# Attention and a mixture of experts on one core: the second half of the queries in two groups of 512 in place of four of 256, their row maxima spread differently, and the last four tiles finished one by one

## The reference

```python
xn  = (x - mean) / sqrt(var + 1e-5)
# attention, one head of width 128, scale 1/sqrt(8)
q, k, v = split(xn @ w_qkv.T)
att = softmax(q @ k.T * scale) @ v @ w_proj.T + b_proj
# experts: 8, each row goes to 2 of them
t = xn @ W_in + b_in
probs = softmax(t @ W_gate + b_gate);  top 2, renormalised
mid  = relu(t @ W1[e] + b1[e])           # 128 -> 512
eout = mid @ W2[e] + b2[e]               # 512 -> 128
ffn  = (sum over the 2 experts of gate * eout) @ W_out + b_out
out  = x + att + ffn
```

## Time and profile before

| | |
|---|---|
| median of 3 runs | 240.3 us (240.28 to 240.36) |
| the profiled execution | 240.15 us |
| its span, first to last record | 238.1 us |
| PE, DVE, ACT, POOL busy in the span | 227.0, 137.3, 111.0, 140.9 us |
| granted TensorE clock | full in all 40 slices |

### The profile page before, as it was taken

How to read it: one execution, slowest core, us unless ns; L and a number is a source line. 1 busy time by engine, 2 the same in 40 slices (tenths; PEclk the granted TensorE clock), 3 DMA queues, 4 the chain that set the end, 5 groups by cost and what they waited for, 6 DMA issues and landing times.

```text
span 238.1 us, 4830 instructions
## 1 busy us (share of the span) xinstructions
PE 227.0 (95%) x1724; PEld 215.1 (90%) x1724; DVE 137.3 (58%) x334; ACT 111.0 (47%) x265; POOL 140.9 (59%) x163
## 2 busy tenths in 40 slices
PE   8899988999999999899999999999899999999985
PEld 8787876899999997899999999999899899999983
DVE  4978795652551541444444444444677885985652
ACT  2572432424325334344444444444656656566561
POOL 3149005888888850355666665563178888888710
PEclk9999999999999999999999999999999999999999
DMA  6799910111111103022222222221111112213111
GB/s 182 285 320 342 323 44 28 49 37 47 34 44 47 44 33 88 25 61 71 71 66 70 77 71 70 76 66 37 33 47 34 44 36 80 43 36 88 53 38 44
DMA packets 23047, 19.54 MB, mean 82 GB/s; under 512 B 3280, under 2 KB 19696, under 8 KB 22768
## 3 DMA queue, kind: packets, MB, share of 16 engines
q1 hardware_dynamic: 20000, 14.71, 20.3%
q0 software_dynamic: 2048, 4.20, 6.4%
q10 hardware_dynamic: 976, 0.33, 0.5%
HBM read 10.97 MB, written 8.26 MB: 81 GB/s over the span
## 4 chain that ended last, share of the span: by engine, by line
PE 57%; POOL 21%; DVE 7%; issue 7%; DMA 5%; ACT 1%; ACTq 1%; POOLq 0%; DVEq 0%
PE ps L1088 15%; PE ps L1074 15%; POOL slots_in L360 12%; POOL wtab L387 4%; POOL x_sb L333 3%; DVE part_max L611 2%; PE ps L890 2%; PE ps L963 2%; PE ps L829 2%; PE ps L964 2%; PE ps L967 2%; DMA w_raw<-in_L_attn_w_proj_dram 2%; PE ps L830 2%; PE ps L831 2%; PE ps L1062 2%
## 5 line engine op out<-in xcount | busy, mean ns | idle before, releaser
L350 POOL COPY wst<-wtab 128x1156 f32 x39 | 44.9, 1151 | 36.0 <-DVE y_sb L759 36.0
L460 ACT ACTIVATE pf<-ps 128x512 f32<-128x512 f32 x64 | 38.1, 595 | 34.5 <-PE ps L831 31.0
L611 DVE TENSOR_REDUCE part_max<-ps 128x1 f32<-128x1024 f32 x32 | 38.9, 1223 | 11.4 <-PE ps L890 10.4
L387 POOL DMA_INDIRECT wtab<-slots_out,slots x32 | 34.5, 1077 | 16.0 <-DMA slots_out<-y_sb 8.4
L360 POOL DMA_INDIRECT slots_in<-hl,slots x32 | 31.5, 984 | 20.1 <-DVE slots L691 13.2
L751 DVE TENSOR_SCALAR mid<-ps,wst 128x128 f32<-128x128 f32 x78 | 23.8, 347 | 33.3 <-PE ps L1074 33.3
L1088 PE MATMUL ps<-wst,mid 128*128 128x128 f32 x312 | 41.3, 275 | 0.7 <-DVE x_sb L638 0.7
L829 PE MATMUL ps<-q_hi,xnT_hi 128*128 128x256 f32 x128 | 41.4, 323 | 0.5 <-ACT q_hi L446 0.5
L1074 PE MATMUL ps<-xgT,wst 128*128 128x128 f32 x312 | 41.3, 275 | 0.0
L1088 PEld LDWEIGHTS ps<-wst,mid 128*128 128x128 f32 x312 | 38.0, 192 | 0.8 <-ACT mid L504 0.8
L1074 PEld LDWEIGHTS ps<-xgT,wst 128*128 128x128 f32 x312 | 38.0, 192 | 0.1
(11 more groups left out here) (158 smaller groups left out, 341.5 us busy)
## 6 DMA issues: line engine op xcount, KB each, us to landing
wtab<-in_L_ffn_W_dram SPq DMA_DIRECT2D x16, 256.0 KB, 6.0
xg<-slots_in SPq DMA_DIRECT2D x39, 64.0 KB, 1.9
slots_out<-y_sb SPq DMA_DIRECT2D x39, 64.0 KB, 1.5
slots_in<-wst SPq DMA_DIRECT2D x2, 1024.0 KB, 5.0
x_sb<-in_L_attn_x_dram SPq DMA_DIRECT2D x4, 256.0 KB, 4.7
out_dram<-x_sb SPq DMA_DIRECT2D x3, 256.0 KB
wtab<-in_L_ffn_b_dram SPq DMA_DIRECT2D x1, 512.0 KB, 7.4
slots_in<-hl,slots POOLq DMA_INDIRECT x32
```

The source lines that it names most:

```text
L350: pool.tensor_copy(wst[:, t % 4, :], wtab[:, bass.ds(experts[t], 1), :].rearrange("p a n -> p (a n)")).then_inc(Z["staged"], 1)
L387: pool.indirect_dma_start(out=z[:, j, c, :], out_offset=None, in_=slots_out, in_offset=bass.IndirectOffsetOnAxis(ap=slots[:, c, j:j + 1], ...
L460: act.activation(pf[:, i % 3, :], ps[:, st_bank(i), :], ACT.Exp).then_inc(Z["pf_done"], 1)
L611: dve.tensor_reduce(part_max[:, g % 2, m // 2, m % 2:m % 2 + 1], ps[:, b:b + 2, :], AX.XY, ALU.max).then_inc(Z["max_read"], 1)
```

## The change

Groups 4 to 7 (256 queries, 8 steps each) become groups 4 and 5 (512 queries, 16 steps each). The number of steps behind the experts stays 32, and so does the number of pairs in the whole kernel (32); a step's six score products of 256 columns become three of 512, and so do those of `values`. The eight pairs of group 4 are now all made in the steps of group 3, one to a step and two in its last; their `max_row` and `row` stand beside expert tile 3. Behind the experts eight pairs are left where twelve were. `combine(j)` and the blocks have new steps: `combine` 14 and 15 and the last block's transposes stand behind all `values`. The last group's tiles (four instead of two) are scaled, projected and added one at a time, each onto its share of the experts' product in the same PSUM bank, and DVE copies `cT` there instead of ACT.

```diff
@@ -36,11 +36,11 @@
-    GROUPS = [(256 * g, 256) for g in range(8)]
+    GROUPS = [(256 * g, 256) for g in range(4)] + [(1024, 512), (1536, 512)]
     PRE = 4
     WHOLE = 4
-    PAIR_STEP = [[2, 4, 5, 6]] + 6 * [[1, 2, 4, 5]] + [[]]
+    PAIR_STEP = [[2, 4, 5, 6]] + 2 * [[1, 2, 4, 5]] + [[1, 2, 3, 4, 5, 6, 7, 7], [1, 3, 5, 6, 8, 9, 11, 12], []]
     NG = len(GROUPS)
     SIZE = [n for _, n in GROUPS]
     CH = [BK // n for n in SIZE]
@@ -72,9 +72,9 @@
     def weighed_at(s):
-        return [j for j in range(NT) if 4 + (13 * (j + 1)) // 8 == s]
-    BLOCK_AT = {14: 0, 22: 1, 26: 2, 31: 3}
+        return [j for j in range(NT) if 5 + (31 * j) // 16 == s]
+    BLOCK_AT = {14: 0, 21: 1, 28: 2}
     ctx = ExitStack()
     with ctx:
@@ -216,11 +216,12 @@
             return ps[:, b:b + 2, 0:2 * HW].rearrange("p b (j n) -> p b j n", n=HW)
         def row_bank(c):
-            return (MA, 0)[c]
+            return (MA, 0, 1, 2)[c]
         def sum_bank(c):
-            return (MB, 1)[c]
+            return (MB, MX + 1, MA, 0)[c]
         def y_bank(t):
             return UB if t % 2 == 0 else MB
@@ -277,11 +278,15 @@
                 store_y(t)
             ov = out.rearrange("o (p j) e -> p (o j) e", p=P)
-            cuts = [TB * r for r in range(NR)] + [GROUPS[NG - 1][0] // P, NT]
+            cuts = [TB * r for r in range(NR)]
             for a, b in zip(cuts, cuts[1:]):
                 sp.wait_ge(Z["moe_added"], (b - 1) // TB + 1)
                 sp.wait_ge(Z["x_added"], sum(q < P * b for q, _ in GROUPS))
                 sp.dma_start(ov[:, a:b, :], x_sb[:, a:b, :]).then_inc(Z["stored"], 16)
+            for c in (2, 4):
+                sp.wait_ge(Z["last_added"], c)
+                a = NT - TB + c - 2
+                sp.dma_start(ov[:, a:a + 2, :], x_sb[:, a:a + 2, :]).then_inc(Z["stored"], 16)
             sp.wait_ge(Z["stored"], 16 * (NR + 1))
         @block.gpsimd
@@ -478,7 +483,7 @@
                     copy_u(g - 1)
             def before(g, k):
-                if k == STEPS[g] - 1 and g + 1 < NG:
+                if k == STEPS[g] - 1 and g + 1 < NG and g != PRE - 1:
                     row(g + 1)
             for g in range(PRE):
@@ -516,6 +521,8 @@
                     mid_relu(t + 1)
                 else:
                     step(BASE_B)
+                if t == 3:
+                    row(PRE)
             def cT_copy(b):
                 act.wait_ge(Z["cT_done"], b + 1)
@@ -800,27 +807,36 @@
                         combine(j)
                     if s - 1 in BLOCK_AT:
                         moe_add(BLOCK_AT[s - 1])
+            for j in range(NT):
+                if j not in [q for s in range(LAST - BASE_B) for q in weighed_at(s)]:
+                    combine(j)
+            dve.wait_ge(Z["cT_done"], NR)
+            dve.wait_ge(Z["wo_done"], NR - 1)
+            dve.tensor_copy(cT[:, :], ps[:, MX, :]).then_inc(Z["cT_copied"], 1)
             def last_scale(c):
-                n = FIRST_ROUND[NG] - 1
+                n = FIRST_ROUND[NG - 1]
                 dve.wait_ge(Z["out_done"], n + 1 + c)
-                link("rinv", dve.reciprocal(rinv[:, n % 2, c:c + 1], ps[:, row_bank(c), D:D + 1]))
-                dve.tensor_scalar(o_sb[:, n % 2, c, :], ps[:, row_bank(c), 0:D], rinv[:, n % 2, c:c + 1], None,
+                link("rinv", dve.reciprocal(rinv[:, c // 2, c % 2:c % 2 + 1], ps[:, row_bank(c), D:D + 1]))
+                dve.tensor_scalar(o_sb[:, c // 2, c % 2, :], ps[:, row_bank(c), 0:D], rinv[:, c // 2, c % 2:c % 2 + 1], None,
                                   ALU.mult).then_inc(Z["o_ready"], 1)
             def last_add(c):
-                at = x_sb[:, NT - 2 + c, :]
-                dve.wait_ge(Z["proj_done"], FIRST_ROUND[NG] + c)
-                return dve.tensor_tensor(at, ps[:, sum_bank(c), 0:D], at, ALU.add)
-            dve.wait_ge(Z["proj_done"], FIRST_ROUND[NG] - 1)
+                at = x_sb[:, NT - TB + c, :]
+                dve.wait_ge(Z["proj_done"], FIRST_ROUND[NG - 1] + c + 1)
+                dve.tensor_tensor(at, ps[:, sum_bank(c), 0:D], at, ALU.add).then_inc(Z["last_added"], 1)
+            dve.wait_ge(Z["proj_done"], FIRST_ROUND[NG - 1])
+            dve.wait_ge(Z["x_biased"], 1 + NT)
             last_scale(0)
             last_scale(1)
-            dve.wait_ge(Z["wo_done"], NR)
-            at = x_sb[:, NT - TB:NT - 2, :]
-            dve.tensor_tensor(at, ps[:, MX + 1, 0:2 * D].rearrange("p (j e) -> p j e", e=D), at, ALU.add).then_inc(Z["moe_added"], 1)
+            last_scale(2)
             last_add(0)
-            last_add(1).then_inc(Z["x_added"], 1)
+            last_scale(3)
+            last_add(1)
+            last_add(2)
+            last_add(3)
         @block.tensor
         def _(pe):
@@ -975,10 +991,7 @@
                 pe.wait_ge(Z["ut_copied"], g + 1)
                 if n >= 1:
                     pe.wait_ge(Z["o_ready"], n)
-                if g == PRE - 1:
-                    pe.wait_ge(Z["row_ready"], PRE + 1)
-                else:
-                    pe.wait_ge(Z["q_lo_ready"], min(NG, g + 3))
+                pe.wait_ge(Z["q_lo_ready"], PRE + 1 if g == PRE - 1 else min(NG, g + 3))
                 for k in range(2):
                     at = P * (2 * r + k)
                     last = pe.matmul(ps[:, MA, (D + 2) * k:(D + 2) * (k + 1)], ut[:, at:at + P], wvT[:, :], start=True, stop=True)
@@ -1089,8 +1102,8 @@
                                      start=(c == 0), stop=(c == HC - 1))
                 last.then_inc(Z["y_done"], 1)
+            values(BASE_B - 2)
             xg_transpose(0)
-            values(BASE_B - 2)
             xg_transpose(1)
             values(BASE_B - 1)
             layer1(0)
@@ -1109,6 +1122,9 @@
                 if t == 1:
                     for r in range(ROUNDS[PRE - 1]):
                         project(PRE - 1, r)
+                if t == 3:
+                    pe.wait_ge(Z["o_ready"], FIRST_ROUND[PRE])
+                    max_row(PRE)
                 layer2(t)
             def moe_transpose(b, pairs):
@@ -1149,25 +1165,25 @@
                         after(g, k)
             values(LAST - 2)
             values(LAST - 1)
-            pe.wait_ge(Z["cT_copied"], NR)
+            moe_transpose(NR - 1, FIRST_PAIR[NG])
+            n = FIRST_ROUND[NG - 1]
+            pe.wait_ge(Z["pf_done"], LAST)
             pe.wait_ge(Z["x_added"], NG - 1)
-            pe.wait_ge(Z["pf_done"], LAST)
-            for c in range(2):
-                at = P * (TB - 2 + c)
-                pe.matmul(ps[:, sum_bank(c), 0:D], cT[:, at:at + P], wo_sb[:, :], start=True, stop=False)
-            for c in range(2):
+            for c in range(TB):
                 pe.wait_ge(Z["ut_copied"], NG + c)
                 pe.matmul(ps[:, row_bank(c), 0:D + 2], ut[:, P * c:P * (c + 1)], wvT[:, :], start=True, stop=True
                           ).then_inc(Z["out_done"], 1)
+            pe.wait_ge(Z["cT_copied"], NR)
             pe.wait_ge(Z["moe_added"], NR - 1)
-            for j in range(TB - 2):
-                last = pe.matmul(ps[:, MX + 1, P * j:P * (j + 1)], cT[:, P * j:P * (j + 1)], wo_sb[:, :], start=True, stop=True)
-            last.then_inc(Z["wo_done"], 1)
-            for c in range(2):
-                n = FIRST_ROUND[NG] - 1
+            for c in range(TB):
+                if c >= 2:
+                    pe.wait_ge(Z["o_ready"], n + c - 1)
+                pe.matmul(ps[:, sum_bank(c), 0:D], cT[:, P * c:P * (c + 1)], wo_sb[:, :], start=True, stop=False)
+            for c in range(TB):
                 pe.wait_ge(Z["o_ready"], n + 1 + c)
-                pe.matmul(ps[:, sum_bank(c), 0:D], o_sb[:, n % 2, c, :], wpT[:, :], start=False, stop=True
+                pe.matmul(ps[:, sum_bank(c), 0:D], o_sb[:, c // 2, c % 2, :], wpT[:, :], start=False, stop=True
                           ).then_inc(Z["proj_done"], 1)
```

2 lines of the change are left out of this document (1 added, 1 removed).

## The result

The changed kernel takes **240.8 us** (20 executions, 240.34 to 242.12) where the kernel before takes 240.3 on the same chip (20 executions, 240.01 to 240.72): ratio 1.0035, interval 1.0022 to 1.0049. It is slower by about 0.5 us; forecast were 241.2 and "slower". The 20 times fall in two groups, 12 from 240.34 to 240.99 and 8 from 241.59 to 242.12; the times of before have no second group. The profiled execution took 240.99 us, of the lower group, with a span of 239.2.

What follows compares the result with a forecast made beforehand. Two chains from the experts' end, TensorE's 64 us and GpSimd's 55 us, meet in the last block. Transposes at 231.5 plus a 5.0 tail give 236.5, +0.9; span 239.0 plus 2.05 is 241.05, median 241.2, range 239.9 to 242.4.

Steps and rivals of the forecast that it cites:

- Before the experts, +3.25: Before the experts: four more pairs in group 3's steps, new waits, wider projection, no max_row; +3.25 us, between +2.3 and +3.7.
- The three new waits: Group 3's last step: second pair waits 0.64 us, first transpose waits for the last reduction, second for ScalarE's copy, 0.70.
- Beside tile 3, +0.45: Beside expert tile 3: four transposes of 128 columns add 0.45 us to TensorE; ScalarE's copy of the row is hidden.
- The list of gathers: GpSimd's list behind the experts starts 3.7 us later, so its last weighing ends at 231.0 instead of 227.32.
- the rival in which the gathers quicken: Behind the experts: slow gathers vanish, 2.5 us go, TensorE alone decides; time 239.9 us, chance 0.15.
- the one in which weighings lengthen: GpSimd and VectorE collide more: half of the 16 weighings become like the longest, chain grows 3.3 us; 244.5, chance 0.05.
- TensorE behind the experts, -5.1: Behind the experts: wider products, fewer pairs, projections and rounds save TensorE 5.1 us; its values end at a stated 231.1.
- the waits cancel: TensorE behind the experts: 3.9 us of waits and slow restarts before, 3.6 counted after, so nearly no change.
- Where both meet: Last block: combine(15) can start at 231.1, last transposes at 231.5; TensorE has been free since 231.1.
- The tail, +5.0: From the last transposes to the last addition: about 5.0 us (4.5 to 5.6), against 5.77 before.
- Sum: Whole kernel: last addition at 236.5 against 235.62, +0.9; span 239.0, with 2.05 around it 241.05; time 241.2 us.
- the rival in which the gathers no longer decide: Same rival as the gathers quickening: TensorE alone decides, values done at about 230.1; time 239.9 us, chance 0.15.

Runs made afterwards that it cites:

- Experiments 1 and 2: Changed kernel with four of eight pairs before the experts cut to 128 columns: 237.96 us; with both last values of group 3 ahead of the first expert transpose: 239.63 us.
- experiment 11: Changed kernel with only the last copy of cT on ScalarE instead of VectorE: 240.71 us, ratio 1.0024.
- experiment 6: Changed kernel without GpSimd's multiplications by the first gate; GpSimd fills a tile of its own after each pair of gathers: 238.21 us, ratio 0.9916.
- experiment 12: Changed kernel with transposes of tiles 12 to 14 ahead of the wait for combine(15) and repeated four times: 240.43 us, ratio 1.0009.

## Why the prediction was right, point by point

The sign, the size and the mechanism held; the terms, one by one:

- **Before the experts, +3.25.** Measured 96.01 - 92.47 = 3.54, of which 0.13 is there already when group 3 starts its first step. The three new waits came as described, 0.45, 0.55 and 0.46 us. Experiments 1 and 2 show that this stretch passes to the end nearly one for one.
- **Beside tile 3, +0.45.** The four transposes took 0.44 from start to start of their neighbours. The first gather came at 175.92, forecast "near 175.7".
- **The list of gathers.** Ends at 231.49, forecast 231.0: 0.25 from its start and 0.22 from its length. The right length is in part luck. The 32 gathers took 33.3 us and not 34.5 (mean 1040 ns against 1077 in the earlier trace rows), 1.2 less; the 16 weighings took 12.35 us together and not 11.57 (median 760 ns against 637), 0.8 more; and the wait for the last rows to land was 1.89 and not 1.08, 0.8 more. So half of the rival in which the gathers quicken (2.5 us) and a quarter of the one in which weighings lengthen (3.3) came true and nearly cancelled. I didn't try what lengthens a weighing.
- **TensorE behind the experts, -5.1.** Mis-sized. The forecast's own terms give 232.65 + 3.7 - 5.1 - 0.3 = 230.95 and not the 231.1 that it states. `values` ended at 232.00 - 1.61 = 230.39, although the stage began 0.25 later than forecast: 0.8 us sooner than the terms say. A product of 512 columns takes 0.227 us from start to start, not 0.23 to 0.234: three of them are 0.68 and not 0.70, which over the 63 half steps is 1.3 us more. The pitch was taken from a pair, whose two products include the change from and to other operands. The waits were named wrongly: the copy of U held `values` for 0.76 (forecast 1.2), one pair waited 0.90 (forecast 1.0 behind `combine(1)`, and a share of another 1.0), the last `low` took 0.24 (0.35). That is 1.9 of the 3.6 that were counted. The rest is slow restarts: if I add up by how much the distances between starts exceed 0.227, 0.120 and 0.110 us (512, 256 and at most 130 columns), waits and restarts come to some 4.1 us here, without the wait for `combine(15)`, and to some 4.5 before. So "the waits cancel" held in the sum (-0.4, forecast -0.3) and not in the parts. Some 0.6 us the other way is left in pairs, projections and short products, which I didn't follow one by one.
- **Where both meet.** TensorE idle for `combine(15)` just before the last transposes, as forecast, but for 1.61 us and not 0.4, because TensorE was sooner and GpSimd later. The transposes started at 232.00, forecast 231.5.
- **The tail, +5.0.** Measured 4.74, with the copy of `cT` at 0.69 (taken: 0.65). The first scaling could start before the copy's listed end.
- **Sum.** Last addition 236.74 against 235.62: +1.1, forecast +0.9. The span is 239.2, forecast 239.0: 0.25 and 0.22 too short in GpSimd's list, 0.26 too long in the tail. The time is 0.4 below the forecast all the same, by two terms outside the span. What lies around the span is 1.79 us and not the 2.05 taken over from the kernel before (see experiment 11), and the profiled execution lies 0.19 above the median and not 0.15 below: 239.2 + 1.79 - 0.19 = 240.8.

Two things came out otherwise than the text had it. First, the rival in which the gathers no longer decide was priced at 239.9; experiment 6 shows 238.2, since TensorE alone is done sooner (last transposes at 229.38, where the rival had `values` end at about 230.1). GpSimd's list therefore costs this version 2.4 us and not 1.3. Second, the median of 240.8 holds something the forecast hadn't: in 8 of 20 executions the idle wait is followed by half the clock in the tail, which adds 1.3 us. Without it the change costs 0.3 us in the median of the lower group (240.6), or 0.2 in experiment 12.

## What to carry to other kernels

A saving behind a stage is worth nothing if a second engine's list starts at the same point and is nearly as long; so before work is moved ahead of that point, compare both lists, because a shift there is paid nearly in full (here 4.0 us, for a saving of TensorE's that was forecast at 5). Where an engine must wait at the end of a kernel, place independent work of TensorE in the wait, and look at all execution times and not only at one profile: a second group of times was the sign. And an experiment that leaves work out may make another engine issue faster; if it gets slower, put an idle filler of the same length in its place.
